# Second attention of a four-stage transformer kernel: rotary columns of two heads per query matmul, and scores as sums over 64 rows

## What is computed

```python
x = x + _L0_attn_ref(_L0_cond_ref(x, ...), L0_attn_Wqkv, L0_attn_Wo)
x = x + _L0_ffn_ref(_L0_cond2_ref(x, ...), ...)
x = x + _L1_attn_ref(_L1_cond_ref(x, ...), L1_attn_wq_a, L1_attn_q_a_ln_w, L1_attn_wq_b, ...)
x = x + _L1_ffn_ref(_L1_cond2_ref(x, ...), ...)
```

```python
q = _rmsnorm(x @ wq_a.T, q_a_ln_w) @ wq_b.T          # 128 latents -> 32 heads x 128
q_nope, q_pe = (q[..., :NOPE], q[..., NOPE:])
ckv, k_pe = (ckv_kpe[..., :KVR], ckv_kpe[..., KVR:]) # ckv_kpe = x @ wkv_a.T
kv = _rmsnorm(ckv, kv_a_ln_w) @ wkv_b.T
k_nope, v = (kv[..., :NOPE], kv[..., NOPE:])
q_pe = _apply_rope(_deinterleave(q_pe), cos, sin)    # x * cos + rotate_half(x) * sin
k_pe = _apply_rope(_deinterleave(k_pe), cos, sin)
scores = jnp.einsum('bqhd,bkhd->bhqk', q_full, k_full) * softmax_scale
attn = jax.nn.softmax(jnp.where(causal, scores, min), axis=-1)
out = jnp.einsum('bhqk,bkhd->bqhd', attn, v) @ wo.T
```

## Time and profile before

| | |
|---|---|
| median of 3 runs | 1078.85 us (1077.42 to 1079.92) |
| the profiled execution, its own time | 1076.43 us |
| its span, first to last instruction | 1074.6 us (1.8 us lie around it) |
| TensorE busy | 979.5 us, 91% of the span |
| VectorE, GpSimd, ScalarE busy | 557.6, 436.7, 224.2 us |
| mean granted TensorE clock | 0.969 of 2.4 GHz |
| attention1, from its first latent query tile to its output product | 798.97 to 931.38 us: 132.4 us |
| spacing of groups in its middle (875.21 to 888.41) | 13.2 us |

### The profile page before, as it was taken

How to read it: one execution, slowest core, us unless ns; L and a number is a source line. 1 busy time by engine, 2 the same in 40 slices (tenths; PEclk the granted TensorE clock), 3 DMA queues, 4 the chain that set the end, 5 groups by cost and what they waited for, 6 DMA issues and landing times.

```text
span 1074.6 us, 15679 instructions
## 1 busy us (share of the span) xinstructions
PE 979.5 (91%) x6684; PEld 706.0 (66%) x6684; DVE 557.6 (52%) x937; ACT 224.2 (21%) x411; POOL 436.7 (41%) x385
## 2 busy tenths in 40 slices
PE   2698769899999999999999879989989999699997
PEld 1233668688888888888888658836854556445953
DVE  4754446566628483666629434344237968301423
ACT  4400210321121212121121120110051566500001
POOL 7997344738446562648347211201212434200300
PEclk9899889999999999999999989999999999799999
DMA  9098110111111110111111941396450000390002
GB/s 246 1 209 241 71 54 1 40 69 41 50 40 69 38 51 1 40 69 40 50 40 58 228 107 68 63 229 131 186 221 1 2 2 2 69 206 1 2 2 79
DMA packets 37998, 83.73 MB, mean 78 GB/s; under 512 B 13412, under 2 KB 22052, under 8 KB 34724
## 3 DMA queue, kind: packets, MB, share of 16 engines
q1 hardware_dynamic: 37736, 81.94, 28.1%
q10 hardware_dynamic: 192, 0.79, 0.3%
HBM read 72.56 MB, written 10.16 MB: 77 GB/s over the span
## 4 chain that ended last, share of the span: by engine, by line
PE 82%; DVE 8%; DMA 3%; ACT 2%; issue 2%; POOL 2%; SPq 0%; POOLq 0%; DVEq 0%; ACTq 0%
PE ps L1091 20%; PE ps L1153 17%; PE ps L989 6%; PE ps L1392 5%; PE ps L1220 5%; PE ps L1324 5%; PE ps L1105 4%; PE ps L1225 1%; PE ps L1138 1%; PE ps L1351 1%; PE ps L1345 1%; PE ps L1332 1%; PE ps L1119 1%; PE ps L1260 1%; PE ps L1364 1%
## 5 line engine op out<-in xcount | busy, mean ns | idle before, releaser
L2285 POOL TENSOR_TENSOR arena<-arena 128x512 f32<-128x512 f32 x80 | 103.6, 1296 | 162.1 <-DVE arena L1876 162.0
L1091 PE MATMUL ps<-xt_hi,w_hi 128*128 128x512 f32 x320 | 128.2, 401 | 11.3 <-issue 8.5
L1091 PE MATMUL ps<-xt_lo,w_hi 128*128 128x512 f32 x320 | 126.7, 396 | 0.0
L1091 PE MATMUL ps<-xt_hi,w_lo 128*128 128x512 f32 x320 | 125.9, 393 | 0.0
L2218 POOL TENSOR_TENSOR xt<-arena 128x512 f32<-128x512 f32 x24 | 30.5, 1272 | 210.3 <-DVE arena L1782 210.3
L1153 PE MATMUL ps<-h_hi,wo_hi 128*128 128x512 f32 x256 | 104.9, 410 | 10.7 <-DVE h_lo L1885 10.7
L1876 DVE TENSOR_TENSOR arena<-ps,rope 64x512 f32<-64x512 f32 x160 | 110.2, 689 | 2.2
L1894 DVE TENSOR_TENSOR fresh<-ps,fresh 128x512 f32<-128x512 f32 x56 | 38.7, 692 | 139.4 <-PE ps L1153 139.4
L1153 PE MATMUL ps<-h_lo,wo_hi 128*128 128x512 f32 x256 | 103.7, 405 | 0.0
L1153 PE MATMUL ps<-h_hi,wo_lo 128*128 128x512 f32 x256 | 103.1, 403 | 0.0
L1091 PEld LDWEIGHTS ps<-xt_hi,w_hi 128*128 128x128 f32 x320 | 60.6, 189 | 27.8 <-issue 10.1
(11 more groups left out here) (303 smaller groups left out, 1795.2 us busy)
## 6 DMA issues: line engine op xcount, KB each, us to landing
arena<-kernel_rows SPq DMA_DIRECT2D x20, 512.0 KB, 18.7
acts<-in_w_o_dram SPq DMA_DIRECT2D x8, 1024.0 KB, 5.0
w_l<-kernel_rows SPq DMA_DIRECT2D x16, 512.0 KB, 14.3
arena<-in_a_wo_dram SPq DMA_DIRECT2D x8, 1024.0 KB, 6.4
acts<-in_w_qkv_dram SPq DMA_DIRECT2D x4, 1792.0 KB, 7.1
acts<-in_w_qkv_dram SPq DMA_DIRECT2D x4, 1280.0 KB, 6.6
arena<-level_rows SPq DMA_DIRECT2D x4, 1024.0 KB, 30.3
kernel_rows<-fresh SPq DMA_DIRECT2D x2, 1536.0 KB, 11.1
```

Of the source, the lines that this page charges most:

```text
L1091: last = pe.matmul(ps[:, bank, :], w[:, r, cols], x, start=(r == 0 and n == 0), stop=(r == R - 1 and n == 2))
L2285: pool.tensor_tensor(qk[:, chunk, half * HALF:(half + 1) * HALF], rot[:, k % 2, 0, :], rot[:, k % 2, 1, :], ALU.add).then_inc(s_rope, 1)
```

## The change

Weights wq1 keep each head's 64 rotary columns once, and one query matmul makes the tile of two heads (rows 0 to 63 and 64 to 127): 4 tiles for a group in place of 8. VectorE multiplies each tile with two tables, cos and sin, into two of the four slots of q1: 8 products for a group, as before, and the ring bank is free after the second. The rotary keys are kept twice, plain (keys_t) and with halves swapped and one sign turned (keys_s), each on rows 0 to 63 and again on rows 64 to 127; ScalarE makes the plain ones in 4 copies of 64 rows (before: 2 of 128 rows), VectorE the swapped ones in 4 copies.

Scores are then sums over 64 rows: for each sample, each of two head pairs' members u and each of the two key forms one matmul of 64 rows x 32 key columns against 64 columns (two heads, 32 tokens). The member u = 0 lies on rows 0 to 63 and writes bank 3, u = 1 on rows 64 to 127 and writes bank 4. That is 8 x 2 x 4 x 2 = 128 rotary matmuls for a group (before: 32, of 128 columns), and 64 latent ones of 64 columns (before: 32 of 128). The bank is now chosen by u, not by the half, so scores(i) waits for both pulls of the group before, pv for both spreads, spread for both halves of pv. In the softmax both subtractions are on GpSimd; maxima follow product 0, sums product 1, turns product 3. Three weight loads on SP's queue (1024, 512 and 512 KB) become one of 1024 KB, and the table rope1c doubles to 32 KB.

```diff
@@ -188,7 +188,7 @@
     cos, sin = (x.T for x in yarn_tables())
-    return np.concatenate([cos, cos, -sin, sin]).astype(np.float32)
+    return np.concatenate([np.tile(cos, (R, 1)), np.tile(sin, (R, 1))], 1).astype(np.float32)
 class Chain:
...
@@ -417,7 +417,8 @@
 att1 = Region()
-wq1 = att1.take(NH, 2 * ROT)
+wq1 = att1.take(NH, ROT)
+keys_s = att1.take(TOK)
 a1_in = att1.take(R, QA + QK1)
...
@@ -660,14 +661,14 @@
     ring1_tile(("l", 0, n), s1_lat, n + 1)
-for k in range(16):
-    ring1_tile(("q", k // 8, k % 8), s1_rot, k + 1)
+for k in range(8):
+    ring1_tile(("q", k // 4, k % 4), s1_rot, k + 1)
 for i in range(8):
             ring1_tile(("l", 1, n), s1_lat, 8 + n + 1)
-    for k in range(8 if i + 2 < 8 else 0):
-        ring1_tile(("q", i + 2, k), s1_rot, 8 * (i + 2) + k + 1)
+    for k in range(4 if i + 2 < 8 else 0):
+        ring1_tile(("q", i + 2, k), s1_rot, 4 * (i + 2) + k + 1)
 def latent(i):
...
@@ -843,12 +844,10 @@
 sp.dma_start(a1_in, a["a1_in"]).then_inc(s1_w, 16)
-sp.dma_start(wq1[:, :, 0:ROT], a["a1_pe"]).then_inc(s1_w, 16)
-sp.dma_start(wq1[:, :, ROT:ROT + ROT // 2], a["a1_pe"][:, :, ROT // 2:ROT]).then_inc(s1_w, 16)
-sp.dma_start(wq1[:, :, ROT + ROT // 2:2 * ROT], a["a1_pe"][:, :, 0:ROT // 2]).then_inc(s1_w, 16)
+sp.dma_start(wq1, a["a1_pe"]).then_inc(s1_w, 16)
 sp.dma_start(a1_ln[:, 0, :], a["a1_ln"]).then_inc(s1_w, 16)
 sp.dma_start(rope1r, a["rope1r"]).then_inc(s1_w, 16)
-sp.dma_start(rope1c, a["rope1c"]).then_inc(s1_w, 16)
+sp.dma_start(rope1c, a["rope1c"].rearrange("p (a c) -> p a c", a=2)).then_inc(s1_w, 16)
 sp.wait_ge(s_back[1], NGROUP)
...
@@ -1320,9 +1319,10 @@
         bank = ring(("q", i, k))
-        g, half = k // 2, k % 2
-        pe.matmul(ps[:, bank, :], wq1[:, GQ * i + g, :],
-                  qa_t[:, half * HALF:(half + 1) * HALF], start=True, stop=True).then_inc(s1_q, 1)
+        pair, half = k // 2, k % 2
+        w = wq1[:, GQ * i + 2 * pair:GQ * i + 2 * pair + 2, :].rearrange("p h n -> p (h n)")
+        pe.matmul(ps[:, bank, :], w, qa_t[:, half * HALF:(half + 1) * HALF],
+                  start=True, stop=True).then_inc(s1_q, 1)
 def latent_queries(four):
...
@@ -1333,29 +1333,32 @@
 def scores(i):
-    rows = slice(32 * (i % 4), 32 * (i % 4) + 32)
-    pe.wait_ge(s1_rot, 8 * (i + 1))
+    low = slice(32 * (i % 4), 32 * (i % 4) + 32)
+    made = q1[i % 2].rearrange("d (p a) n -> d a p n", a=2)
+    pe.wait_ge(s1_rot, 4 * (i + 1))
     pe.wait_ge(s1_lat, 8 * (i // 4 + 1))
-    for t in range(2):
-        if i:
-            pe.wait_ge(s_pull, SOFT0 + 2 * (i - 1) + t + 1)
-        for m in range(4):
+    if i:
+        pe.wait_ge(s_pull, SOFT0 + 2 * i)
+    for q in range(NTILE):
+        for n, keys in enumerate((keys_t, keys_s)):
             for j in range(G):
-                b = (4 * t + m) * G + j
-                pe.matmul(ps[32 * j:32 * j + 32, 3 + t, m * P:(m + 1) * P],
-                          keys_t[:, b * C:(b + 1) * C], q1[i % 2][:, :, b * C:(b + 1) * C],
-                          start=(m == 0), stop=True, skip_group_check=True)
-        for m in range(4):
+                toks = slice((q * G + j) * C, (q * G + j + 1) * C)
+                for u in range(2):
+                    rows = slice(64 * u, 64 * u + 64)
+                    pe.matmul(ps[32 * j:32 * j + 32, 3 + u, q * 64:(q + 1) * 64],
+                              keys[rows, toks], made[rows, n, :, toks],
+                              start=(q == 0 and n == 0), stop=True, skip_group_check=True)
+    for u in range(2):
+        for q in range(NTILE):
             for j in range(G):
-                b = (4 * t + m) * G + j
-                last = pe.matmul(ps[32 * j:32 * j + 32, 3 + t, m * P:(m + 1) * P],
-                                 keys_l[rows, b * C:(b + 1) * C], q_lat[rows, :, b * C:(b + 1) * C],
-                                 **ADD)
+                toks = slice((q * G + j) * C, (q * G + j + 1) * C)
+                last = pe.matmul(ps[32 * j:32 * j + 32, 3 + u, q * 64:(q + 1) * 64],
+                                 keys_l[low, toks], q_lat[low, u:GQ:2, toks], **ADD)
         last.then_inc(s_score, 1)
     for half in range(2):
-        pe.wait_ge(s1_place, 2 * i + half + 1)
+        pe.wait_ge(s1_place, 2 * i + 2)
         if i:
...
@@ -1366,22 +1369,23 @@
         last.then_inc(s1_pv, 1)
-pe.wait_ge(s1_turnc, 6)
+pe.wait_ge(s1_turnc, 8)
+pe.wait_ge(s1_turnd, 4)
 pe.wait_ge(s1_wcc, 8)
 latent_queries(0)
-queries(0, range(8))
-queries(1, range(8))
+queries(0, range(4))
+queries(1, range(4))
 scores(0)
     if i + 2 < 8:
-        queries(i + 2, range(5))
+        queries(i + 2, range(3))
     if i:
     if i + 2 < 8:
-        queries(i + 2, range(5, 8))
+        queries(i + 2, range(3, 4))
     if i + 1 < 8:
...
@@ -1579,11 +1583,14 @@
                    scale=a1_ln[:, 0, 0:1]).then_inc(s1_turnc, 1)
-for q in range(4):
+for q in range(2):
     act.wait_ge(s1_turn, q + 3)
-    dst = (keys_t, keys_l)[q // 2]
-    act.activation(dst[:, q % 2 * HALF:(q % 2 + 1) * HALF], ps[:, 2 + q, :], ACT.Copy)\
-        .then_inc(s1_turnc, 1)
+    for u in range(2):
+        act.activation(keys_t[64 * u:64 * u + 64, q * HALF:(q + 1) * HALF], ps[0:64, 2 + q, :], ACT.Copy)\
+            .then_inc(s1_turnc, 1)
+for q in range(2):
+    act.wait_ge(s1_turn, q + 5)
+    act.activation(keys_l[:, q * HALF:(q + 1) * HALF], ps[:, 4 + q, :], ACT.Copy).then_inc(s1_turnc, 1)
 def latents_in(four):
...
@@ -1596,23 +1603,20 @@
     for t in range(2):
-        if t == 0:
-            act.wait_ge(s_shift, SOFT0 + i + 1)
-        else:
-            act.wait_ge(s1_shift, i + 1)
+        act.wait_ge(s_shift, SOFT0 + 2 * i + t + 1)
         x = probs1[:, i % 2, t].rearrange("p a b -> p (a b)")
         act.activation(x, x, ACT.Exp, scale=R1_SCALE).then_inc(s_exp, 1)
-def spread(i, t):
-    act.wait_ge(s1_flat, 2 * i + t + 1)
+def spread(i, u):
+    act.wait_ge(s1_flat, 2 * i + u + 1)
     if i:
-        act.wait_ge(s1_pv, 2 * (i - 1) + t + 1)
+        act.wait_ge(s1_pv, 2 * (i - 1) + 2)
     for j in range(G):
         q = slice(32 * j, 32 * j + 32)
-        last = act.activation(probs1_t[q, 4 * t:4 * t + 4, :, j, :].rearrange("p a g q -> p (a g) q"),
-                              flat[q, t, :, :], ACT.Copy)
+        last = act.activation(probs1_t[q, :, u:GQ:2, j, :],
+                              flat[q, u, :, :].rearrange("k (a p) q -> k a p q", p=2), ACT.Copy)
     last.then_inc(s1_place, 1)
...
@@ -2075,9 +2079,10 @@
 ch.wait()
+dve.tensor_tensor(keys_n[:, :, 0:32], parts[0], parts[1], ALU.subtract)
 for n in range(2):
-    dve.tensor_tensor(keys_n[:, :, 64 * n:64 * n + 32], parts[0], parts[1], ALU.subtract)
-    dve.tensor_tensor(keys_n[:, :, 64 * n + 32:64 * n + 64], parts[2], parts[3], ALU.add)
+    dve.tensor_tensor(keys_n[:, :, 32 + 32 * n:64 + 32 * n], parts[2], parts[3], ALU.add)
+dve.tensor_tensor(keys_n[:, :, 96:128], parts[1], parts[0], ALU.subtract)
 dve.wait_ge(s1_root, 2)
...
@@ -2086,15 +2091,24 @@
 dve.tensor_copy(lat_n, values1.unsqueeze(2).broadcast_to([P, NTILE, G, LAT])).then_inc(s1_kn, 1)
+for q in range(2):
+    dve.wait_ge(s1_turn, q + 3)
+    for u in range(2):
+        dve.tensor_copy(keys_s[64 * u:64 * u + 64, q * HALF:(q + 1) * HALF], ps[64:128, 2 + q, :])\
+            .then_inc(s1_turnd, 1)
 def rotate(i, k):
-    dve.wait_ge(s1_q, 8 * i + k + 1)
+    dve.wait_ge(s1_q, 4 * i + k + 1)
     if i >= 2 and k == 0:
     x = ps[:, ring1_at["q", i, k], :].rearrange("p (b s) -> p b s", s=C)
-    y = q1[i % 2][:, k // 2, k % 2 * HALF:(k % 2 + 1) * HALF].rearrange("p (b s) -> p b s", s=C)
-    dve.tensor_tensor(y, x, rope1c[:, :].unsqueeze(1).broadcast_to([P, HALF // C, C]), ALU.mult)\
-        .then_inc(s1_rot, 1)
+    for n in range(2):
+        y = q1[i % 2][:, 2 * (k // 2) + n, k % 2 * HALF:(k % 2 + 1) * HALF]\
+            .rearrange("p (b s) -> p b s", s=C)
+        last = dve.tensor_tensor(y, x, rope1c[:, n, :].unsqueeze(1).broadcast_to([P, HALF // C, C]),
+                                 ALU.mult)
+    last.then_inc(s1_rot, 1)
 dve.wait_ge(s1_wc, 8)
...
@@ -2106,26 +2120,22 @@
                       probs1[:, i % 2, t].rearrange("p a b -> p (a b)")).then_inc(s1_flat, 1)
-for k in range(16):
-    rotate(k // 8, k % 8)
+for k in range(8):
+    rotate(k // 4, k % 4)
 for i in range(8):
     soft_pull(i, SOFT0, p)
-    for k in range(8):
+    for k in range(4):
         if i + 2 < 8:
             rotate(i + 2, k)
+        if k == 0:
+            soft_max(i, SOFT0, p, stat1)
         if k == 1:
-            soft_max(i, SOFT0, p, stat1)
-            dve.wait_ge(s_max, SOFT0 + 2 * i + 2)
-            dve.tensor_tensor(p[:, 1], p[:, 1], stat1[:, 1, 0, :].unsqueeze(2)
-                              .broadcast_to([P, 16, C]), ALU.subtract).then_inc(s1_shift, 1)
+            soft_sum(i, SOFT0, p, stat1)
         if k == 3:
-            soft_sum(i, SOFT0, p, stat1)
-        if k == 6:
             turn_flat(i)
...
@@ -2272,7 +2282,7 @@
 soft_mask(i, SOFT0, p)
-soft_shift(i, SOFT0, p, stat1, (0,))
```

(9 more changed lines are left out.)

## The result

The changed kernel takes 1107.95 us (median of 4 runs, 1107.47 to 1108.65) against 1079.38 of the kernel before in the same session: ratio 1.0268, 95% interval 1.0250 to 1.0285. It is 2.7% slower; 1068.4 was forecast, and the range ended at 1079.5.

What follows compares the result with a forecast made beforehand. TensorE was taken to bound the middle, at 13.2 us a group. Laid out -15.1, front +1.0, end +0.7 and clock +3.0 give -10.4 us, so 1078.85 becomes 1068.4 us, range 1061 to 1079.5.

Steps and rivals of the forecast that it cites:

- Query tiles, -3.4 a group: In each group on TensorE, 8 query tiles become 4 at 0.858 us each, taking 3.43 us away.
- Scores: the unknown price: TensorE's 384 score records a group: 2.2 us rotary plus 1.9 latent, 4.1 in all, as much as before.
- The clock, +3.0, bounds 0 and +8: Half clock for pv and half the scores behind two TensorE idle stretches, before pv(0) and pv(5): +1.5 us each.
- The sign I had named: Granted clock below 0.95 between 830 and 900 us, which would show the clock falling in many groups.
- the 120 I had laid out: From first latent tile to the end: 116.4 us laid out, +0.7 for the last pv halves, +3.0 for the clock.
- The loop of spreads at 11.3 us: Spreads, pv, last query tile, products and turn form a loop over three engines that holds each group's period: 11.3 us.
- In front +1.0: Ahead of the loop ScalarE makes six copies after the queries' two, not four, at 0.5 us: +1.0 us.
- VectorE, spreads, products, DMAs at nothing: VectorE at 10.6 us a group is not the latest; spreads and products keep their times; dropped DMA loads are worth nothing.
- scores(0) 7 us sooner after the first latent tile: At the start 16 query tiles become 8, so scores(0) can start 6.9 us earlier.
- Rival 1: Every TensorE record costs 27 ns on average whatever its columns: scores 10.7 us a group, total 1104; chance 0.12.
- Rivals 2 and 3: Scores in the array: halved columns save nothing, 1078, chance 0.10; row halves don't run beside each other, 1073, chance 0.10.
- Rival 4: TensorE idle 1 to 2 us a group drops its clock in many groups: 14.5 us a group, 1086; chance 0.05.

Runs made afterwards that it cites:

- before_coarse_waits: The kernel before with only the softmax side of the change, its coarser waits and both subtractions on GpSimd; 1080.15 us, ratio 1.0017 to before.
- latent_whole_early: latent_whole with the first latent tiles started before the key copies end and VectorE subtracting the last tile's maximum; 1074.96 us, ratio 0.9984 to before.
- latent_whole: The kernel after with 128-column latent matmuls (64 a group), half-tile waits, two query tiles inside scores and earlier turns; 1076.72 us, ratio 0.9984 to before.
- before_split: The kernel before with every score matmul cut into two of 64 columns, 256 instead of 128 records a group; 1090.90 us, ratio 1.0121 to before.
- after_wide: The kernel after with each rotary score matmul taking 128 columns in place of 64, same count of instructions; 1101.95 us (one run).

## Why the prediction was wrong

- *Query tiles, -3.4 a group*: right in records, L1324 has 64 in the loop and not 128. In time the loop got half, -13.8 of -26.9: the tiles that are left ran mostly at 1.2 GHz.
- *"Scores: the unknown price"*: the size was nearly right, 2.2 + 1.9 us against 2.7 + 2.2 at full clock (256 at 10.5 ns; 61 latent records start in the 1.06 us from 929.62, 17 ns each). That a record is handed out much faster than one in 27 ns holds. It is 0.8 us a group, 6 in all.
- *The step that failed is what is missing in that part and in the sum*: the supply of instructions. I counted columns, records, weight loads and tile shapes, but not 768 instructions for scores against what arrives: +26.4 us of issue. The forecast's group of 10.5 to 12 us became one of 16.7. The trace of before shows how near the edge it is: scores there use 256 instructions in 4.06 us, which the new kernel's supply just gives.
- *The clock, +3.0, bounds 0 and +8*: that it falls where TensorE stands still was right, the size wrong, since most of the idle was missing from the sum. At the prices of full clock the tiles lost 39.9 - 26.9 = 13.0 us, the latent tiles 1.6, the score records 49.0 - 8 x 4.9 = some 10: about 25, as much as the gaps. The sign I had named showed: the clock is 0.81 between 830 and 900 us.
- Gaps, clock and record price sum to some 57 us, the loop is only 41 over the 120 I had laid out (116.4, +0.7, +3.0): 3 of clock were in it, and 1.5 us a group in which TensorE would have waited for the spreads, which its own delays now cover.
- *The loop of spreads at 11.3 us*: not late in the changed kernel (before_coarse_waits: 1.0017), but it shows in a stretch of latent_whole_early, where TensorE is faster. Its size was not measured: latent_whole, with earlier turns and the half waits of before, has groups of 11.2 us without a wait for it.
- *In front +1.0*: the first latent tile came 3.3 us later. before_split, whose front is that of before, has it at 800.99 where the profiled execution of before had 798.97; against that the change cost 1.3: the transposes of the head part start at 796.06 in before_split and at 796.04 in the kernel after. The other 2.0 us are the clock, and no part of the change: from 788.2 to 798.3 us it was 0.50 in the kernel after and in before_split, and 1.00 in the profiled execution of before.
- *VectorE, spreads, products, DMAs at nothing*: right. VectorE is busy 84.9 us of the loop against 92.5, ScalarE 69.4 in both, and a spread takes 0.629 us for 0.627.
- *scores(0) 7 us sooner after the first latent tile*: 816.46 - 802.30 = 14.2 against 20.9: right, 6.7.
- *Rivals.* Rival 1 gave 1104, near the result, for a reason that the runs refute: no record costs 27 ns, they take 9 to 17. The Trainium skill's 25 ns between starts ("TensorE: Matmul & The Clock Gate", section "Wait — 56ns, not 53.3ns?"), weighed there for 1097, is refuted for different tiles by the same rows. Rivals 2 and 3 fall with after_wide: twice the columns, no slower. (Rival 3's sum adds 3 us where the forecast adds 4.7, without a reason; nothing hangs on it.) Rival 4 was half of the truth, 1086 with 0.05: the clock did fall in many groups, but behind idle that it did not have.

The group from 905.19, by what was measured: pv 1.9, tiles 3.4, score records 4.9, issue 2.6, half clock on tiles 2.5 and on scores 1.4: 16.7 us. With the supply in the sum a forecast would have had 3.6 blocks a group at 3.3 to 4.1 us: 12 to 15 us if all were spread evenly, more as three of them lie in scores, ahead of any loss to the clock; so hardly a gain at best.

What stays open: the split of the 28.6 us between gaps and clock is worked out from rows, not shown by a run. Short gaps did leave the clock alone: before_split has gaps of 0.4 to 0.7 us, and one of 1.07 at the very end, between 826 and 904 us, latent_whole of 0.4 to 0.8 between 842 and 904, both at 1.00. But no kernel had gaps as long as the changed one's without a fall. That a block comes in 3.3 to 4.1 us is made of the packet and the times before and after it (above); what sets these, and whether a kernel can change them, was not tried.

## What to carry to other kernels

Count TensorE's instructions (a matmul of 32-bit floats is four here) in each stretch, not only its columns: over 256 in 3.3 to 4.1 us can't be kept up, and a split that halves columns doubles them. If a stretch has more, put long matmuls between the short ones, so that each 256 instructions hold about 4 us of work (ratio 1.0139 to 0.9984 here, with the turns moved too), before taking work away. Gaps that the profile calls "issue", a multiple of 256 of the engine's instructions apart (its separate semaphore waits counted), are this.
